# Second norm: inverse deviations of three token tiles made in one step behind the last unit's scaling, and their normalisation moved behind the loop over units

## The chip, the cores and the metric

One Trainium2 chip, of which the kernel uses one core. The metric is the device time in microseconds (us) of a run; the kernel before has a median of 427.91 us over 3 runs (426.51 to 429.72).

## The reference

The input is 16 images of 96 channels and 16 x 16 pixels. Three parts follow each other:

- a masked convolution from input to gates, then a recurrence over the 16 rows (per row a width-3 convolution of the hidden state, sigmoids, a cell `c = f*c + i*g`, `h = o*tanh(c)`), a 1x1 skip convolution and a residual;
- attention on the 256 tokens of each image, causal (6 heads of 16), on `_ln_t(t)`, with a residual: `t = t + attn(_ln_t(t))`;
- a mixture of 4 experts (96 to 384 to 96, exact gelu, top 2 of 4 by softmax) on `_ln_t(t)` of the new `t`, with a residual.

The norm before the experts is what the change touches. For each token over its 96 channels:

```
def _ln_t(v, eps=1e-05):
    m = jnp.mean(v, axis=-1, keepdims=True)
    s = jnp.var(v, axis=-1, keepdims=True)
    return (v - m) / jnp.sqrt(s + eps)
```

## The kernel before

**Tiling.** After the recurrence (the first 64 us or so) the tokens are worked through in 8 blocks (`NBLK`) of 512, each in 4 tiles (`SPB`) of 128 tokens. Attention of a block is cut into 10 units (`NU`), a unit being a few heads of one tile of queries. Units 0, 1 belong to tile 0 (three heads, 128 keys), units 2, 3, 4 to tile 1 (two heads, 256 keys), units 5, 6 to tile 2 (as tile 0), units 7, 8, 9 to tile 3 (as tile 1). `TILE_END` is [2, 5, 7, 10].

**A unit's way through the engines.** TensorE (PE) makes the scores in one of two banks `S` (`scores`, L1068 to L1073). VectorE (DVE) takes the row maximum (`row_max`, L792). ScalarE (ACT) makes the exponentials and their sums (`exps`, L598). DVE inverts the sums (`recip`, L798). GpSimd (POOL) multiplies the exponentials by them in place (`scale`, L453, one instruction for each head). PE transposes the result into the one bank `T` (`probs_t`, L1084), and ACT or DVE copies it out (`take_pt`, L502; ACT for units 1, 2, 4, 6, 8, 9, DVE for 0, 3, 5, 7). PE multiplies with the values into bank `A` (`values`, L1105) in slots 2, 5, 7 and behind the loop. `probs_t(u)` waits both for `scale(u)` and for the copy of unit u-1, since `T` is one bank.

**A tile's way after its last unit.** ACT copies `A` out (`heads_out`, L607), PE projects (`project_out`, L1111), DVE adds the residual and makes mean and variance (`attn_residual`, L805, L807, L809), POOL makes the inverse deviation (`rstd2`: an addition, L436, and a power of -1/2, L438), and DVE normalises (`normalize2`, L813). When all four tiles are there, PE transposes them (L1215), ACT and DVE split the result into two parts (`x2hi`, L639, and `x2lo`, L914), and the hidden layer of the experts runs (`expert_hidden`, L1142 to L1146, with the gelu on ACT, L644). The experts' second product of a block (`expert_out`, L1126) is spread as filling over the slots of the next block's attention (`FILL`), and DVE weighs it (`combine`, L870).

**Order.** Everything is written out by hand, and each engine executes its own list in order, with semaphores between them. One pass of the unit loop is slot j. On POOL, slot j holds `scale(n, j + 1)`; slot 2 also `rstd1(n + 1)` (the first norm of the next block, L430 and L432, all four tiles in one step); slots 3, 6 and 8 also `rstd2(n, 0)`, `rstd2(n, 1)`, `rstd2(n, 2)`, behind the scaling of that slot and so in front of `scale(n, 5)`, `scale(n, 8)` and, for tile 2, of nothing more. `rstd2(n, 3)`, `keep_t1`, `residual` and `x1_whole` follow behind the loop. On DVE, slot j holds `row_max(n, j + 2)`, `recip(n, j + 1)`, perhaps `take_pt`, `combine` and the first norm's work, `attn_residual` of tiles 0, 1, 2 in slots 3, 6, 8 and `normalize2` of the same tiles in slots 4, 7, 9. Behind the loop stand `combine(n - 1, 2)`, `attn_residual(n, 3)`, `q_rest`, `normalize2(n, 3)`, `k_rest`, `x2lo` and the rest. On PE, behind the loop: `project_q`, the values of units 7, 8, 9, `project_k`, `project_out(n, 3)`, nine parts of `expert_out`, then the transposes of L1215.

The first block (`first=True`) has no `expert_out` and no `combine` as filling; in some places PE runs matmuls there whose result nobody reads (`keep_clock`, L1008), but not in slots 3 to 9. The last block has no projection for a next block.

Of the kernel before, what the change touches and what calls it, by code (L numbers as in the profile page):

```python
# [23 lines left out]
ALU = mybir.AluOpType  # L24
# [14 lines left out]
SPB = 4  # L39
# [13 lines left out]
TILE_END = [1 + max(u for u, (a, t, _) in enumerate(UNITS) if 2 * a + t == s) for s in range(SPB)]  # L53
# [11 lines left out]
def hybrid_kernel(nc, x, w_input, w_state, b_skip, wq, wk, wv, wp, bp,  # L65
                  gate_w, gate_b, w1, b1, w2, b2, ident, ident_bf, causal_bf, lower, out):
    with ExitStack() as ctx:
        def sb(name, shape, dt=F32):
            return ctx.enter_context(nc.sbuf_tensor(name, shape, dt))
# [4 lines left out]
        def sem(name):  # L74
            return ctx.enter_context(nc.semaphore(name))
# [38 lines left out]
        nhalf = sb("nhalf", [128, SPB])  # L114
# [39 lines left out]
        mv2 = sb("mv2", [128, SPB, 2])  # L154
        ve2 = sb("ve2", [128, SPB])
        rs2 = sb("rs2", [128, SPB])
# [83 lines left out]
        ln2_aggr = sem("ln2_aggr")  # L240
# [6 lines left out]
        rs2_step = sem("rs2_step")  # L247
# [36 lines left out]
        def wait_alone(eng, semaphore, value):  # L284


            if not isinstance(value, int):
                value = eng.snap(eng.to_reg(value))
            eng.wait_ge(zeroed, N_ZEROED)
            eng.wait_ge(semaphore, value)  # L290
# [124 lines left out]
        @block.gpsimd  # L415
        def _(pool):
            nc.gpsimd.memset(h_pad[:], 0.0).then_inc(zeroed, 1)
            nc.gpsimd.memset(gate[:, :, 2], 0.0).then_inc(zeroed, 1)
            nc.gpsimd.memset(h_tok[:], 0.0).then_inc(zeroed, 1)
            nc.gpsimd.memset(as_f32(k_bd[:]), 0.0).then_inc(zeroed, 1)  # L420
            nc.gpsimd.memset(v_cur[:], 0.0).then_inc(zeroed, 1)
            nc.gpsimd.memset(nhalf[:], -0.5).then_inc(zeroed, 1)
            nc.gpsimd.memset(as_f32(ones2[:]), 0.0).then_inc(zeroed, 1)
            nc.gpsimd.memset(as_f32(b2hl[:]), 0.0).then_inc(zeroed, 1)
            pool.wait_ge(zeroed, N_ZEROED)

            def rstd1(n):

                wait_alone(pool, ln1_aggr, 4 * n + 4)
                nc.gpsimd.tensor_scalar(ve1[:], mv1[:, :, 1], 1e-5, None, ALU.add).then_inc(rs1_step, 1)  # L430
                pool.wait_ge(rs1_step, 2 * n + 1)
                nc.gpsimd.tensor_tensor(rs1[:], ve1[:], nhalf[:], ALU.pow).then_inc(rs1_step, 1)  # L432

            def rstd2(n, s):
                wait_alone(pool, ln2_aggr, 4 * n + s + 1)
                nc.gpsimd.tensor_scalar(ve2[:, s:s + 1], mv2[:, s, 1:2], 1e-5, None, ALU.add).then_inc(rs2_step, 1)  # L436
                pool.wait_ge(rs2_step, 8 * n + 2 * s + 1)
                nc.gpsimd.tensor_tensor(rs2[:, s:s + 1], ve2[:, s:s + 1], nhalf[:, 0:1], ALU.pow).then_inc(rs2_step, 1)  # L438

            def residual(n):  # L440

                pool.wait_ge(t0_done, n + 1)
                nc.gpsimd.tensor_tensor(tb[:], t0[:], bp_sb[:].unsqueeze(1).to_broadcast((128, SPB, C)),
                                        ALU.add).then_inc(tb_done, 1)

            def scale(n, u):

                wait_alone(pool, rden_done, NU * n + u + 1)
                _, t, _ = UNITS[u]
                nk = TT * (t + 1)  # L450
                for i in range(HG[t]):
                    p = p_sb[:, u % 3, i * nk:(i + 1) * nk]
                    last = nc.gpsimd.tensor_scalar(p, p, rden[:, u % 3, i:i + 1], 1.0, ALU.mult, ALU.mult)  # L453
                last.then_inc(scaled, 1)

            def x1_whole(n):

                wait_alone(pool, x1lo_done, n + 1)
                nc.gpsimd.tensor_tensor(x1f[:], as_f32(x1hi[:]), as_f32(x1lo[:]), ALU.add).then_inc(x1f_done, 1)

            def keep_t1(n, first):

                wait_alone(pool, t1_done, 4 * n + 4)
                if not first:
                    wait_alone(pool, comb, 16 * n)
                nc.gpsimd.tensor_copy(t1p[:], t1[:]).then_inc(t1p_done, 1)

            def body(n, first=False, last=False):
                scale(n, 0)
                for j in range(NU):  # L470
                    if j + 1 < NU:
                        scale(n, j + 1)
                    if j == EARLY_T0 + 1 and not last:
                        rstd1(n + 1)
                    for s in range(SPB - 1):
                        if j == TILE_END[s] + 1:
                            rstd2(n, s)
                rstd2(n, SPB - 1)
                keep_t1(n, first)
                if not last:  # L480
                    residual(n + 1)
                    x1_whole(n + 1)

            pool.wait_ge(w_in, 16 * N_WIN)
            rstd1(0)
            x1_whole(0)
            load_keys(nc.gpsimd, 0, 1, 0)
            residual(0)
            body(0, first=True)
            with pool.Fori(1, NBLK - 1) as n:  # L490
                body(n)
            body(NBLK - 1, last=True)
# [176 lines left out]
        def _(dve):  # L669
# [139 lines left out]
                V.bn_aggr(mv2[:, s], st2[:, s]).then_inc(ln2_aggr, 1)  # L809

            def normalize2(n, s):
                dve.wait_ge(rs2_step, 8 * n + 2 * s + 2)
                V.tensor_scalar(xh2[:, s], t1[:, s], mv2[:, s, 0:1], rs2[:, s:s + 1],  # L813
                                ALU.subtract, ALU.mult).then_inc(xh2_done, 1)

# [45 lines left out]
            def combine(n, s, first):  # L861

                dve.wait_ge(y_ready, 4 * n + s + 1)
                dve.wait_ge(t1p_done, n + 1)
                if s == 0 and not first:
                    dve.wait_ge(y_out, 16 * n)
                for e in range(E):
                    if e:
                        dve.wait_ge(comb, 16 * n + 4 * s + e)
                    V.scalar_tensor_tensor(y_sb[:, s], L2[s][:, e * C:(e + 1) * C], gw[:, s, e:e + 1],  # L870
                                           t1p[:, s] if e == 0 else y_sb[:, s], ALU.mult, ALU.add).then_inc(comb, 1)

            def body(n, first=False, second=False, last=False):
                if not first:
                    route(n - 1, 1)
                recip(n, 0)
                if first:
                    row_max(0, 1)
                else:
                    route(n - 1, 2)  # L880
                for j in range(NU):
                    if j + 2 < NU:
                        row_max(n, j + 2)
                    if j + 1 < NU:
                        recip(n, j + 1)
                    if j not in PT_ON_ACT:
                        take_pt(dve, n, j, first)
                    if j == EARLY_XT + 1 and not last:
                        x1_rest(n + 1)
                    if not first and j:  # L890
                        for s, c in out_parts(j - 1):
                            if c == NCH - 1:
                                combine(n - 1, s, second)
                    if not last:
                        if j == EARLY_T0 + 1:
                            norm1(n + 1)
                        if j == EARLY_T0 + 2:
                            normalize1(n + 1)
                    for s in range(SPB - 1):
                        if j == TILE_END[s] + 1:  # L900
                            attn_residual(n, s, first)
                        if j == TILE_END[s] + 2:
                            normalize2(n, s)
                if not first:
                    for s in range(sum(FILL[:-1]) // NCH, sum(FILL) // NCH):
                        combine(n - 1, s, second)
                attn_residual(n, SPB - 1)
                if not last:
                    q_rest(n + 1)
                normalize2(n, SPB - 1)  # L910
                if not last:
                    k_rest(n + 1)
                dve.wait_ge(x2hi_done, n + 1)
                V.tensor_tensor(x2lo[:], T[0:C, :], as_f32(x2hi[:]), ALU.subtract).then_inc(x2lo_done, 1)  # L914
                if not first:
                    for s in range(sum(FILL) // NCH, SPB):
                        combine(n - 1, s, second)
                route(n, 0)
                if not last:
                    row_max(n + 1, 0)  # L920
                    row_max(n + 1, 1)
# [410 lines left out]
```

## Time and profile before

| what | value |
|---|---|
| median of 3 runs | 427.91 us (426.51, 427.91, 429.72) |
| the profiled execution, its time | 431.65 us |
| its span, first to last instruction | 429.7 us |
| granted TensorE clock over the span | 0.987 of full |
| PE, busy | 404.0 us (94%), 3024 matmuls |
| ACT, busy | 267.1 us (62%) |
| DVE, busy | 248.3 us (58%) |
| POOL, busy | 147.6 us (34%) |

An engine's share is its busy time over the span. A steady block of 512 tokens takes 41.69 us (the same instruction of two blocks in a row: 190.54 and 232.23 us for the transposes of unit 8). Block 0 runs from about 85 us on, the last from about 380 us on.

### The profile page before, as it was taken

The page shows a single profiled execution, that of the slowest core. Times are in us where ns is not written, and L with a number is a line of the kernel's source. Part 1 is how long each engine was busy: PE and PEld are TensorE (multiplying, and loading weights), DVE is VectorE, ACT ScalarE, POOL GpSimd, SP SyncE. Part 2 cuts the span into 40 slices and gives each one's busy share as a digit, 9 for nine tenths or more (in the row PEclk, how much of TensorE's full clock was granted, in tenths as well). Part 3 has the DMA queues.
Part 4 walks back from the last instruction along what each step waited for, and adds up shares of the span by engine and source line. Part 5 has one row for each costly group of instructions (what it writes and reads, how often), then busy time and mean ns, then how long its engine had stood idle before and what let it go on. Part 6 is the DMA issues. An engine that isn't in the chain of part 4 may idle for free.

```text
span 429.7 us, 10320 instructions
## 1 busy us (share of the span) xinstructions
PE 404.0 (94%) x3024; PEld 332.1 (77%) x3024; DVE 248.3 (58%) x867; ACT 267.1 (62%) x766; POOL 147.6 (34%) x314
## 2 busy tenths in 40 slices
PE   7999998887999899989998999899989998999996
PEld 4988984555588788868886888789777887787786
DVE  1576774475328753866386548645864585367425
ACT  3566652465486658665865686567747764877380
POOL 6000002366305631563155315532642254236200
PEclk9899999998899999999999999999999999999999
DMA  7700000310111012101200220021002100210000
GB/s 177 177 0 0 0 2 19 83 29 2 43 36 36 2 46 53 30 0 50 55 23 0 54 55 21 0 61 49 18 0 64 46 0 8 76 27 3 7 13 20
DMA packets 16472, 14.87 MB, mean 35 GB/s; under 512 B 7586, under 2 KB 13588, under 8 KB 16452
## 3 DMA queue, kind: packets, MB, share of 16 engines
q1 hardware_dynamic: 14644, 13.74, 12.4%
q10 hardware_dynamic: 1616, 0.74, 0.7%
q8 instruction: 10, 0.16, 0.2%
q0 software_dynamic: 192, 0.15, 0.2%
q14 instruction: 10, 0.08, 0.1%
HBM read 3.80 MB, written 1.57 MB: 12 GB/s over the span
## 4 chain that ended last, share of the span: by engine, by line
PE 72%; DVE 9%; issue 7%; POOL 6%; ACT 3%; DMA 1%; ACTq 1%; SPq 1%; POOLq 0%; DVEq 0%
PE F L1126 14%; PE T L1084 6%; PE A L1105 5%; PE F L1142 5%; PE F L1146 4%; PE F L1143 4%; PE F L957 3%; POOL p_sb L453 3%; PE S L1068 3%; PE S L1070 2%; ACT p_sb L598 2%; PE F L967 2%; DVE xh L770 2%; PE F L968 2%; PE S L1073 2%
## 5 line engine op out<-in xcount | busy, mean ns | idle before, releaser
L453 POOL TENSOR_SCALAR p_sb<-p_sb,rden 128x128 f32<-128x128 f32 (+1 forms) x192 | 79.5, 429 | 115.3 <-DVE rden L798 113.1
L1126 PE MATMUL F<-w_sb,hid 128*128 128x96 f32 x768 | 98.8, 272 | 0.0
L1126 PEld LDWEIGHTS F<-w_sb,hid 128*128 128x128 f32 x768 | 96.1, 192 | 0.0
L598 ACT ACTIVATE p_sb<-S,nmax 128x128 f32<-128x128 f32 (+1 forms) x192 | 78.9, 424 | 11.4 <-DVE nmax L792 11.4
L792 DVE TENSOR_REDUCE nmax<-S 128x2 f32<-128x512 f32 (+1 forms) x80 | 50.6, 632 | 51.5 <-PE S L1073 51.2
L1084 PE MATMUL T<-id_sb,p_sb 128*128 128x128 f32 x288 | 48.1, 286 | 12.3 <-POOL p_sb L453 10.4
L502 ACT COPY pt_sb<-T 128x512 f32<-128x512 f32 (+1 forms) x48 | 26.5, 551 | 44.6 <-PE T L1084 44.6
L644 ACT ACTIVATE hid<-F,b_sb 128x512 f32<-128x512 f32 x72 | 49.4, 689 | 7.0 <-PE F L1146 6.3
L1084 PEld LDWEIGHTS T<-id_sb,p_sb 128*128 128x128 f32 x288 | 31.5, 144 | 21.9 <-POOL p_sb L453 17.7
L598 ACT ACTIVATION_READ_ACCUMULATOR p_sb<-S,nmax 128x1 f32 x192 | 39.7, 207 | 0.0
L1068 PE MATMUL S<-k_bd,q_st 96*128 96x384 f32 (+2 forms) x96 | 38.1, 404 | 1.5 <-ACT p_sb L598 1.1
L870 DVE SCALAR_TENSOR_TENSOR y_sb<-F,gw,y_sb 128x96 f32<-128x96 f32 x96 | 30.5, 318 | 3.4
L1070 PE MATMUL S<-k_bd,q_st 96*128 96x384 f32 (+2 forms) x96 | 31.7, 338 | 0.0
L1142 PE MATMUL F<-x2hi,w1hi 96*128 96x512 f32 x72 | 29.9, 415 | 1.4 <-ACT x2hi L639 0.8
L1146 PE MATMUL F<-x2lo,w1hi 96*128 96x512 f32 x72 | 29.2, 406 | 0.0
L1105 PE MATMUL A<-pt_sb,v_cur 128*32 128x128 f32 x576 | 28.9, 284 | 0.0
L1143 PE MATMUL F<-x2hi,w1lo 96*128 96x512 f32 x72 | 28.5, 396 | 0.0
L502 DVE COPY pt_sb<-T 128x384 f32<-128x384 f32 (+1 forms) x32 | 20.0, 624 | 11.4 <-PE T L1084 11.3
L1073 PE MATMUL S<-causal_sb,idb_sb 128*128 128x256 bf16 (+1 forms) x80 | 24.5, 306 | 0.0
L1105 PEld LDWEIGHTS A<-pt_sb,v_cur 128*32 128x32 f32 x576 | 20.0, 111 | 5.6 <-ACT pt_sb L502 3.0
L430 POOL TENSOR_SCALAR ve<-mv 128x4 f32<-128x4 f32 x8 | 1.9, 239 | 64.6 <-DVE mv L764 64.6
L436 POOL TENSOR_SCALAR ve<-mv 128x1 f32<-128x1 f32 x32 | 7.3, 227 | 46.0 <-DVE mv L809 45.3
(151 smaller groups left out, 789.3 us busy)
## 6 DMA issues: line engine op xcount, KB each, us to landing
k_bd<-k_cur SPq DMA_DIRECT2D x93, 32.0 KB, 2.0
q_st<-q_cur SPq DMA_DIRECT2D x28, 96.0 KB, 2.3
k_bd<-k_cur SPq DMA_DIRECT2D x93, 16.0 KB, 1.8
t_st<-t_cm SPq DMA_DIRECT2D x7, 192.0 KB, 2.5
out_y<-y_sb SPq DMA_DIRECT2D x7, 192.0 KB, 1.9
x_pad<-in_x SPq DMA_DIRECT2D x2, 612.0 KB, 7.4
w_sb<-in_w SPq DMA_DIRECT2D x1, 576.0 KB
hid<-in_w SPq DMA_DIRECT2D x1, 576.0 KB, 6.8
```

The lines of the kernel that those rows point to most:

```text
L453: last = nc.gpsimd.tensor_scalar(p, p, rden[:, u % 3, i:i + 1], 1.0, ALU.mult, ALU.mult)
L502: copy(pt_sb[:, u % NPT, 0:w], T[:, 0:w]).then_inc(pt_done, 1)
L598: last = nc.scalar.activation(p_sb[:, u % 3, i * nk:(i + 1) * nk], S[u % 2][:, i * nk:(i + 1) * nk], ACT.Exp, bias=nmax[:, u % 3, i:i + 1] ...
L644: nc.scalar.activation(hid[:, c, :], L1[c % 4][:], ACT.Gelu, bias=b1_sb[:, c:c + 1]).then_inc(gelu_done, 1)
L792: V.tensor_reduce(nmax[:, u % 3, 0:HG[t]], S[u % 2][:, 0:HG[t] * nk].rearrange("p (h k) -> p h k", k=nk), AX.X, ALU.max, negate=True).then ...
L1068: mm(d, q_st[:, g, ts], k_bd[:, a, 0, g, i0:i1, 0:nk], start=(3 * g + i0 == h0), stop=False, skip_group_check=True)
L1084: last = nc.tensor.transpose(T[:, i * TT:(i + 1) * TT], p_sb[:, u % 3, i * TT:(i + 1) * TT], id_sb[:])
L1105: last = mm(A[VW * (h % 3):VW * (h % 3) + VW, 0:TT], v, pt_sb[:, u % NPT, c0:c0 + TT], start=(kt == 0 and h < 3), stop=(kt == t and h >= 3 ...
L1126: last = mm(dst[:, e * C:(e + 1) * C], hid[:, c, s * TT:(s + 1) * TT], w2_sb[:, c], start=False, stop=(c == NCH - 1), skip_group_check=True)
L1142: mm(dst, w1hi[:, cs], x2hi[:], start=True, stop=False)
L1143: mm(dst, w1lo[:, cs], x2hi[:], start=False, stop=False)
L1146: mm(dst, w1hi[:, cs], x2lo[:], start=False, stop=True).then_inc(hid_ready, 1)
```

## The change

`rstd2` takes a range of tiles instead of one. It is called twice for a block, both times behind the loop over units: for tiles 0 to 2 in one addition and one power of 128 x 3 elements, then for tile 3. The three calls in the loop are gone. It waits for the statistics of the last tile of its range. `rs2_step` counts 4 in a block instead of 8. On DVE `normalize2` of tiles 0, 1 and 2 leaves slots 4, 7 and 9 and stands in a row behind the loop, behind `combine(n - 1, 2)` and in front of `attn_residual(n, 3)`.

```diff
-            def rstd2(n, s):
-                wait_alone(pool, ln2_aggr, 4 * n + s + 1)
-                nc.gpsimd.tensor_scalar(ve2[:, s:s + 1], mv2[:, s, 1:2], 1e-5, None, ALU.add).then_inc(rs2_step, 1)
-                pool.wait_ge(rs2_step, 8 * n + 2 * s + 1)
-                nc.gpsimd.tensor_tensor(rs2[:, s:s + 1], ve2[:, s:s + 1], nhalf[:, 0:1], ALU.pow).then_inc(rs2_step, 1)
+            def rstd2(n, s0, s1):
+
+                wait_alone(pool, ln2_aggr, 4 * n + s1)
+                nc.gpsimd.tensor_scalar(ve2[:, s0:s1], mv2[:, s0:s1, 1], 1e-5, None, ALU.add).then_inc(rs2_step, 1)
+                pool.wait_ge(rs2_step, 4 * n + (3 if s0 else 1))
+                nc.gpsimd.tensor_tensor(rs2[:, s0:s1], ve2[:, s0:s1], nhalf[:, s0:s1], ALU.pow).then_inc(rs2_step, 1)
...
                         rstd1(n + 1)
-                    for s in range(SPB - 1):
-                        if j == TILE_END[s] + 1:
-                            rstd2(n, s)
-                rstd2(n, SPB - 1)
+                rstd2(n, 0, SPB - 1)
+                rstd2(n, SPB - 1, SPB)
                 keep_t1(n, first)
...
             def normalize2(n, s):
-                dve.wait_ge(rs2_step, 8 * n + 2 * s + 2)
+                dve.wait_ge(rs2_step, 4 * n + (4 if s == SPB - 1 else 2))
...
                             attn_residual(n, s, first)
-                        if j == TILE_END[s] + 2:
-                            normalize2(n, s)
                 if not first:
                     for s in range(sum(FILL[:-1]) // NCH, sum(FILL) // NCH):
                         combine(n - 1, s, second)
+                for s in range(SPB - 1):
+                    normalize2(n, s)
                 attn_residual(n, SPB - 1)
```

## Rows read from the trace of the kernel before

**Rows 1.** The page, part 1: busy time, share of the span, instructions.
```profile
PE 404.0 (94%) x3024; PEld 332.1 (77%) x3024; DVE 248.3 (58%) x867; ACT 267.1 (62%) x766; POOL 147.6 (34%) x314
```
**Rows 2.** Waits by line: waiter, releaser, us in total, times, longest us.
```profile
PE T L1084 <- POOL p_sb L453: 10.4, 10, 1.4
...
PE T L1215 <- DVE xh L813: 1.1, 7, 0.2
```
**Rows 3.** The tile rs: times in ns (least/median/most), first and last start.
```profile
L438 POOL TENSOR_TENSOR rs<-ve,nhalf x32: 567/569/579, 96.9 to 402.9; 128x1 f32<-128x1 f32 x32
...
L432 POOL TENSOR_TENSOR rs<-ve,nhalf x8: 1042/1043/1052, 69.9 to 345.8; 128x4 f32<-128x4 f32 x8
```
**Rows 4.** Timeline of POOL, a steady block (start, us, instruction, idle before).
```profile
225.31 1.09 POOL L453 TENSOR_SCALAR p_sb<-p_sb,rden 128x128 f32<-128x128 f32 x3
...
229.23 0.93 POOL L453 TENSOR_SCALAR p_sb<-p_sb,rden 128x256 f32<-128x256 f32 x2 [1.06 <-DVE rden L798]
230.24 0.23 POOL L436 TENSOR_SCALAR ve<-mv 128x1 f32<-128x1 f32 x1
...
231.22 1.87 POOL L453 TENSOR_SCALAR p_sb<-p_sb,rden 128x256 f32<-128x256 f32 x4
```
**Rows 5.** Timeline of the other engines, same block, units 5 to 9.
```profile
226.65 0.31 PEld L1084 LDWEIGHTS T<-id_sb,p_sb 128*128 128x128 f32 x3 [0.20 <-POOL p_sb L453]
...
228.91 0.15 DVE L798 RECIPROCAL rden<-den 128x2 f32<-128x2 f32 x1
...
230.39 0.15 DVE L798 RECIPROCAL rden<-den 128x2 f32<-128x2 f32 x1
...
230.98 0.69 DVE L502 COPY pt_sb<-T 128x512 f32<-128x512 f32 x1 [0.44 <-PE T L1084]
...
231.59 0.32 DVE L813 TENSOR_SCALAR xh<-t,mv,rs 128x96 f32<-128x96 f32 x1
...
232.23 0.66 PE L1084 MATMUL T<-id_sb,p_sb 128*128 128x128 f32 x4 [1.09 <-POOL p_sb L453]
...
232.93 0.59 ACT L502 COPY pt_sb<-T 128x512 f32<-128x512 f32 x1 [1.25 <-PE T L1084]
...
233.62 0.42 PEld L1084 LDWEIGHTS T<-id_sb,p_sb 128*128 128x128 f32 x4 [0.26 <-issue]
```
**Rows 6.** Timeline, same block, behind the loop over units.
```profile
233.78 0.18 DVE L809 BATCH_NORM_AGGREGATE mv<-st 128x2 f32<-128x6 f32 x1
...
235.63 1.02 DVE L870 SCALAR_TENSOR_TENSOR y_sb<-F,gw,y_sb 128x96 f32<-128x96 f32 x3
...
237.09 0.26 DVE L805 TENSOR_TENSOR t<-M,tb 128x96 f32<-128x96 f32 x1 [0.44 <-PE M L1111]
...
239.39 0.64 PE L1215 MATMUL T<-id_sb,xh 128*96 128x128 f32 x4 [0.15 <-DVE xh L813]
```
**Rows 7.** Timeline of the last block, units 7 and 8.
```profile
396.22 0.69 DVE L502 COPY pt_sb<-T 128x512 f32<-128x512 f32 x1 [0.48 <-PE T L1084]
...
397.23 0.66 PE L1084 MATMUL T<-id_sb,p_sb 128*128 128x128 f32 x4 [0.84 <-POOL p_sb L453]
```
**Rows 8.** Timeline of the first block, units 5 to 8.
```profile
96.73 0.17 DVE L798 RECIPROCAL rden<-den 128x3 f32<-128x3 f32 x1
...
97.53 2.19 POOL L453 TENSOR_SCALAR p_sb<-p_sb,rden 128x128 f32<-128x128 f32 x6
...
98.71 0.55 PE L1084 MATMUL T<-id_sb,p_sb 128*128 128x128 f32 x3 [0.59 <-POOL p_sb L453]
...
102.97 0.69 DVE L502 COPY pt_sb<-T 128x512 f32<-128x512 f32 x1 [0.47 <-PE T L1084]
...
104.35 1.07 PE L1084 MATMUL T<-id_sb,p_sb 128*128 128x128 f32 x4 [1.43 <-POOL p_sb L453]
```
**Rows 9.** Windows, PE: stretch, length, busy (count), granted clock, DMA share, GB/s.
```profile
104.35:111.31 6.96, 6.56 (x40) 0.51 0.00 0
232.23:236.48 4.25, 4.12 (x44) 1.00 0.00 0
```

## The prediction

> **What bounds the kernel now.** I read the busy shares first, then the waits by line, then the timeline of one steady block (190.54 to 232.23 us between the same transposes, 41.69 us), and last the first and the last block. PE is busy for 94% of the span [rows 1], so only its idle time can be won, and its own list must be followed to see what a shift is worth. The waits name one place: the transposes of the scaled probabilities waited 10 times for POOL's scaling, 10.4 us together [rows 2]. In the timeline of a steady block that is unit 8: PE stands still for 1.09 us until 232.23 [rows 5]; the six steady blocks show this pause at 1.09 or 1.10 us. The last block has 0.84 us [rows 7], the first 1.43 us at unit 8 and 0.59 us at unit 5 [rows 8]. The reader should see what POOL does just before: it ends the scaling of unit 7 at 230.16 (229.23 + 0.93), makes the inverse deviation of tile 1 from 230.24 on, and starts the scaling of unit 8 at 231.22 [rows 4], although its reciprocal was done at 230.54 [rows 5]. The small step on one column stands in front of the scaling that PE waits for.
>
> **Part 1, removed from POOL's loop.** One inverse deviation holds POOL from 230.24 to 231.22, 0.98 us from start to start [rows 4]. The two durations alone are 0.23 [rows 4] and 0.57 [rows 3], 0.80 us. The Trainium skill ("Perfetto Trace Analysis", on the profiler's boundary for GPSIMD) advises timing POOL by the spacing of starts; by durations the step would be 0.18 us cheaper. The next terms use starts, and do not need that advice.
>
> Without the step, scaling 8 starts as late behind its reciprocal as scaling 7 does: that reciprocal ended at 229.06, the scaling started at 229.23, 0.17 later [rows 4, 5]. So 230.54 + 0.17 = 230.71, the pair takes 0.93 as in unit 7, and PE follows 0.08 us behind (232.23 against 231.22 + 0.93 = 232.15): 231.72. But the transposes also need bank T, which DVE's copy of unit 7 leaves at 231.67 (230.98 + 0.69); PE needed 0.10 us behind such a copy for unit 9 (233.62 against 232.93 + 0.59) [rows 5]. That gives 231.77, and the gain is 232.23 - 231.77 = **0.46 us**. What is late next is the copy of unit 7, so more than 0.46 can't come from here; the lower bound is 0 if something not seen holds unit 8.
>
> Is it kept? From unit 8 on PE's list is a chain: unit 9's transposes follow the copy of unit 8 by 0.10 us, then come the projections and values without a pause of note, until the residual of tile 3 at 237.09 and the transposes of the norm at 239.39 [rows 6]. All move together, and with them the query and key transfers that DVE releases there. Scaling 9 would run from 231.64 to 232.57, and unit 9's transposes would be due at 233.16: no new wait. Six steady blocks: 6 x 0.46 = **2.8 us**.
>
> In front of unit 5 the step also goes. There the scaling ended at 226.40, PE's transposes began only at 226.65 [rows 4, 5], three times the 0.08 seen behind unit 8, so PE itself set that moment; steady unit 5 counts 0. The last block: the copy of unit 7 ends at 396.91, plus 0.10 is 397.01 against 397.23 [rows 7]: **0.2 us**. The first block has no filling, so both steps cost. Unit 5: reciprocal done at 96.90, plus 0.17 is 97.07 against 97.53, 0.46 us, of which PE waited 0.59 [rows 8]; everything to unit 8 follows that. Unit 8: copy done at 103.66, plus 0.10 is 103.76 against 104.35, 0.59 us more [rows 8]. Together **1.05 us**.
>
> **Part 2, the same work in one step.** A power of four columns takes 1.043 us, of one 0.569 [rows 3]; three lie between, evenly 0.885 us. Bounds 0.57 and 1.04. It follows the statistics of tile 2 at 233.96 [rows 6] and stands behind scaling 9, which is over by then. Taking 0.16 us to start and 0.31 for the addition (0.98 less 0.67 for the power with its gap), the result is there at about 235.3. Behind it on POOL waits only tile 3's own step, whose statistics come some 2.6 us later. Cost on the path: 0, covered by PE's values and projections.
>
> **Part 3, three normalisations on DVE.** 0.32 us each [rows 5], some 0.95 in a row. DVE now ends the weighing of tile 2 at 236.65 and then idles 0.44 until the projection of tile 3 at 237.09 [rows 6]. Tile 2's normalisation no longer stands in front of that weighing with its wait for POOL, so the weighing (four instructions, three of them 1.02 us [rows 6], 1.4 us with the first) starts at 233.96 and ends near 235.4, the three normalisations near 236.35, and some 0.75 us stay before 237.09; the shift of part 1 moves all of these alike. Cost 0; upper bound, were none of this room there, 0.5 us in a block (236.65 + 0.95 against 237.09). Taken out of slots 4 and 7, two normalisations free DVE by 0.25 us each, in front of row maxima and reciprocals; DVE idles 0.44 us in front of the copy of unit 7 [rows 5], so I count 0, bound 0.05 us a block from the reciprocal of unit 9.
>
> **The clock.** From 104.35 to 111.31 the granted clock is 0.51, the lower of the two levels (1.2 GHz), after PE stood still for 1.43 us [rows 8, 9]; the same way through the list takes 4.25 us in a steady block at 2.4 GHz [rows 9], although that has the filling as well. The low stretch costs about 2.7 us. The change shortens the pauses in front of it from 0.59 and 1.43 us by 0.46 and 0.59. In a steady block a pause of 1.09 us does not lower the clock. What it gives: 0 if the clock falls anyway, 2.7 if never.
>
> The Trainium skill ("TensorE: Matmul & The Clock Gate", the part on HAM oscillation) says that pauses of PE make the gate lower its clock and that keeping it supplied holds the clock up; by that rule alone the first block would keep 2.4 GHz, and the profile of before agrees as far as the fall goes: 0.51 behind the pause of 1.43 us.
>
> **Sum.** 2.8 + 0.2 + 1.05 = 4.0 us without the clock. The profiled execution took 431.65 us (span 429.7 and 1.95 around it), 3.7 above the median; with the clock kept up it would read 431.65 - 4.0 - 2.7 = 424.9. The runs shown spread over 3.2 us, about what the low stretch costs, so I take the highest to have it whole, the lowest not at all, and the median 427.91 - 426.51 = 1.4 us of it. Forecast 427.91 - 4.0 - 1.4 = **422.5 us**.
>
> **Rivals.**
> - *Clock as before.* The waits go, the low stretch comes as often: 427.91 - 4.0 = 423.9. For it: the pauses get shorter but don't vanish. Chance 0.25.
> - *Clock counts whole.* All runs of before had the low stretch, none after: 427.91 - 6.7 = 421.2. For it: the profiled one has it. Against: its time lies above all runs shown. Chance 0.13.
> - *Hidden anyway.* Another release sets unit 8 or the gain is eaten behind the loop, where PE still waits for the last normalisation 0.15 us [rows 6] (1.1 us in all [rows 2]); half of the 4.0 stays: 425.9. Chance 0.13.
> - *The end is late (slower).* The batched step delays the residual of tile 3. It decides once the inverse deviations are later than 237.09 - 0.95 = 236.14, that is, a batch of over 2.0 us from 234.12. As three single steps it would be 3 x 0.98 = 2.94, done at 237.06, and the residual 0.92 us late in 8 blocks, 7.4 us: 431.3 with the gain of part 1, 435.3 if that fails too. Against it stands the four-column power of 1.043 us [rows 3]. Chance 0.05.
>
> The forecast has 0.44. **The numbers.** One per cent is 4.3 us, about what this kernel's measurement can tell from none; the limit is 423.6. Faster by more: nearly all of the forecast's case and the whole-clock case, a third of the clock-as-before case: 0.6. Within: the rest of that, the hidden case and the slower one with part 1's gain: 0.36. Slower: 0.04. The range goes from 420.7, just below the whole-clock case with 0.05 us a block more, to 426.0, which takes in the half gain.
>
> **What would show it.** Right: in a steady block POOL's scaling of unit 8 starts 0.17 us behind its reciprocal, PE's pause there falls from 1.09 to about 0.6 us and now ends 0.10 us behind DVE's copy of unit 7; the block takes 41.2 us instead of 41.7; one power of 128x3 lasts near 0.89 us; the residual of tile 3 still waits for PE's projection, by about 0.75 us. In the first block the pause at unit 8 is below 0.9 us and no stretch of low clock follows. Wrong: a block still takes 41.7, a wait of the residual's on DVE's own normalisations, or the low clock at another place of the first block.

## The result, and the profile after

The changed kernel takes **424.14 us** (median of 11 runs, 422.45 to 425.27) against 428.10 for the kernel before in runs beside it (11, 426.46 to 432.96): a ratio of 0.9892, 95% interval 0.9867 to 0.9917. The forecast was 422.5 us, in a range of 420.7 to 426.0. It is faster by 1.1%, as forecast, and by 3.96 us of medians where 5.4 had been expected.

The page of the changed kernel, busy time and share of the span (421.1 us; the profiled execution took 423.02 us). It answers to [rows 1]:
```profile
PE 399.7 (95%) x3024; PEld 328.1 (78%) x3024; DVE 249.4 (59%) x867; ACT 266.8 (63%) x766; POOL 137.2 (33%) x282
```
POOL has 32 instructions fewer: two of the three inverse deviations of each of 8 blocks, two instructions each. PE's busy time fell by 4.3 us too although its work is the same: that is the low clock that this execution does not have (granted clock 1.000 over the span, 0.987 before).

Its waits by line (waiter, releaser, us in total, times, longest), against [rows 2]:
```profile
PE T L1083 <- DVE pt_sb L501: 5.6, 8, 0.9
...
PE T L1083 <- POOL p_sb L454: 1.7, 3, 0.9
PE T L1214 <- DVE xh L812: 1.2, 7, 0.2
```
Of 10.4 us behind POOL's scaling 1.7 are left, and 5.6 us stand now behind a releaser that was not in the list for this line: DVE's copy of the unit before.

The tile rs of the changed kernel, against [rows 3] (ns, first and last start):
```profile
L439 POOL TENSOR_TENSOR rs<-ve,nhalf x16: 579/730/887, 103.4 to 394.2; 128x3 f32<-128x3 f32 x8, 128x1 f32<-128x1 f32 x8
```

The timeline of POOL in a steady block, against [rows 4]:
```profile
222.56 0.94 POOL L454 TENSOR_SCALAR p_sb<-p_sb,rden 128x256 f32<-128x256 f32 x2 [1.31 <-DVE rden L797]
224.04 0.93 POOL L454 TENSOR_SCALAR p_sb<-p_sb,rden 128x256 f32<-128x256 f32 x2 [0.55 <-DVE rden L797]
225.37 0.93 POOL L454 TENSOR_SCALAR p_sb<-p_sb,rden 128x256 f32<-128x256 f32 x2 [0.39 <-DVE rden L797]
227.01 0.24 POOL L437 TENSOR_SCALAR ve<-mv 128x3 f32<-128x3 f32 x1 [0.71 <-DVE mv L808]
227.34 0.88 POOL L439 TENSOR_TENSOR rs<-ve,nhalf 128x3 f32<-128x3 f32 x1
```
Three scalings (units 7, 8, 9), each started by its reciprocal, and then the addition and the power of three columns. The other engines in the same block, against [rows 5, 6]:
```profile
223.72 0.16 DVE L797 RECIPROCAL rden<-den 128x2 f32<-128x2 f32 x1
...
224.31 0.69 DVE L501 COPY pt_sb<-T 128x512 f32<-128x512 f32 x1 [0.44 <-PE T L1083]
...
225.15 0.63 PE L1083 MATMUL T<-id_sb,p_sb 128*128 128x128 f32 x4 [0.68 <-DVE pt_sb L501]
...
226.55 0.63 PE L1083 MATMUL T<-id_sb,p_sb 128*128 128x128 f32 x4
...
226.67 0.18 DVE L808 BATCH_NORM_AGGREGATE mv<-st 128x2 f32<-128x6 f32 x1
...
227.20 1.02 DVE L869 SCALAR_TENSOR_TENSOR y_sb<-F,gw,y_sb 128x96 f32<-128x96 f32 x3
228.25 0.81 DVE L812 TENSOR_SCALAR xh<-t,mv,rs 128x96 f32<-128x96 f32 x3
229.99 0.26 DVE L804 TENSOR_TENSOR t<-M,tb 128x96 f32<-128x96 f32 x1 [0.93 <-PE M L1110]
```
The scaling of unit 8 is done at 224.97 (224.04 + 0.93), but PE goes on only at 225.15, 0.15 us behind the end of the copy (225.00). The power of three columns and DVE's weighing both end at 228.22, the three normalisations at 229.06, and DVE idles 0.93 us before the residual of tile 3.

The first block, PE's transposes of units 7, 8 and 9, against [rows 8]:
```profile
99.66 0.66 PE L1083 MATMUL T<-id_sb,p_sb 128*128 128x128 f32 x4
101.19 0.63 PE L1083 MATMUL T<-id_sb,p_sb 128*128 128x128 f32 x4 [0.88 <-DVE pt_sb L501]
...
102.63 0.66 PE L1083 MATMUL T<-id_sb,p_sb 128*128 128x128 f32 x4 [0.61 <-POOL p_sb L454]
```
Windows of PE in the changed kernel (stretch, length, busy with count, granted clock, DMA share, GB/s):
```profile
10.00:15.00 5.00, 4.34 (x26) 1.00 1.09 240
15.00:20.00 5.00, 5.00 (x34) 1.00 0.59 163
98.00:104.00 6.00, 4.37 (x37) 1.00 0.00 1
104.00:111.00 7.00, 6.24 (x53) 1.00 0.19 54
```
The same windows of the kernel before, near the start:
```profile
10.00:15.00 5.00, 4.33 (x18) 0.73 1.09 238
15.00:20.00 5.00, 5.00 (x31) 0.93 0.61 172
```
The low stretch of the first block is gone in this execution, but so is one at 10 to 20 us, ahead of anything that the change touches. So the two spans differ by more than the change is worth. To divide the 8.6 us (429.7 against 421.1) I take four marks: the start, the transposes of unit 0 of the first block (87.29 before, 85.20 after), and the first and the last transposes of the norm. In the kernel before:
```profile
114.39 0.42 PE L1215 MATMUL T<-id_sb,xh 128*96 128x128 f32 x2
...
403.85 0.31 PE L1215 MATMUL T<-id_sb,xh 128*96 128x128 f32 x1 [0.20 <-DVE xh L813]
```
and in the changed one, with the second block's between them:
```profile
108.57 0.31 PE L1214 MATMUL T<-id_sb,xh 128*96 128x128 f32 x1
...
149.80 0.31 PE L1214 MATMUL T<-id_sb,xh 128*96 128x128 f32 x1 [0.17 <-DVE xh L812]
...
395.24 0.53 PE L1214 MATMUL T<-id_sb,xh 128*96 128x128 f32 x3 [0.17 <-DVE xh L812]
```
That gives 2.09 us in the start, 27.10 - 23.37 = 3.73 in the first block, 289.46 - 286.67 = 2.79 in the seven that follow, and nothing in the tail (25.85 and 25.86). The first is not the change's. One steady block, between the same marks, takes 41.23 us (149.80 - 108.57) instead of 41.65; over all six it is 41.23 to 41.26 against 41.65 to 41.71.

### The profile page after: what moved, and what is told of

The parts are those of the page before. It is cut to its first block, busy times and chain, and to the rows that moved or that the text cites. A ratio compares the mean times of both kernels' runs of the same rounds, so it can differ in the third digit from the quotient of the medians.

```text
span 421.1 us, 10222 instructions
## 1 busy us (share of the span) xinstructions
PE 399.7 (95%) x3024; PEld 328.1 (78%) x3024; DVE 249.4 (59%) x867; ACT 266.8 (63%) x766; POOL 137.2 (33%) x282
## 4 chain that ended last, share of the span: by engine, by line
PE 82%; DVE 6%; issue 3%; POOL 3%; ACT 2%; DMA 1%; ACTq 1%; SPq 1%; POOLq 0%; DVEq 0%
PE F L1125 16%; PE T L1083 8%; PE A L1104 6%; PE F L1141 5%; PE F L1145 4%; PE S L1067 4%; PE F L1142 4%; PE S L1069 3%; PE F L956 3%; PE S L1072 2%; PE F L966 2%; PE M L1110 2%; PE F L967 2%; DVE pt_sb L501 2%; PE S L972 1%
## 5 line engine op out<-in xcount | busy, mean ns | idle before, releaser
L1083 PE MATMUL T<-id_sb,p_sb 128*128 128x128 f32 x288 | 46.6, 280 | 8.8 <-DVE pt_sb L501 5.6
L1104 PE MATMUL A<-pt_sb,v_cur 128*32 128x128 f32 x576 | 28.0, 278 | 0.0
L1067 PEld LDWEIGHTS S<-k_bd,q_st 96*128 96x128 f32 x96 | 18.2, 190 | 3.6 <-ACT p_sb L597 2.4
```

Source lines behind the costliest of these rows:

```text
L1067: mm(d, q_st[:, g, ts], k_bd[:, a, 0, g, i0:i1, 0:nk], start=(3 * g + i0 == h0), stop=False, skip_group_check=True)
L1083: last = nc.tensor.transpose(T[:, i * TT:(i + 1) * TT], p_sb[:, u % 3, i * TT:(i + 1) * TT], id_sb[:])
L1104: last = mm(A[VW * (h % 3):VW * (h % 3) + VW, 0:TT], v, pt_sb[:, u % NPT, c0:c0 + TT], start=(kt == 0 and h < 3), stop=(kt == t and h >= 3 ...
```

## The experiments

Twelve kernels were run. "At full clock" below means those runs whose granted clock, over the whole run, was at least 0.998 of the higher level. Of 73 runs of the kernel before (a 74th, at 433.48 us, is left out), 27 were such (mean 427.16 us), 24 had 0.993 to 0.997 (428.54) and 22 less (430.29). They come in four sets beside the experiments, whose runs at full clock have means of 427.07 to 427.31. Of 11 runs of the changed kernel 5 were at full clock (422.82), 6 at 0.994 to 0.996 (424.53) and none below. So at full clock the change is worth 4.34 us. The marks of the traces give 3.78 of it, as shown under before_filled; the other half microsecond is not explained. I compare on this footing beside the ratio, because a low stretch costs as much as the differences looked for.

**norm_moved_only.** Half of the change: the kernel before with only the normalisations moved. (The other half can't run by itself: the normalisations must follow POOL's steps.)
```
-                        if j == TILE_END[s] + 2:
-                            normalize2(n, s)
...
+                for s in range(SPB - 1):
+                    normalize2(n, s)
                 attn_residual(n, SPB - 1)
```


> The DVE half of the change alone: the kernel before, with the normalisations of tiles 0 to 2 moved behind the loop, while POOL makes the inverse deviations one by one in its slots as before. Theory (POOL's single step in front of the scaling of unit 8 is what PE pays for, 0.42 us in a steady block by the trace of the changed kernel): nothing moves, the pause in front of unit 8 stays at 1.05 to 1.10 us, median within 0.5 us of the kernel before. Rival (the normalisations in DVE's slots, in front of row maxima and reciprocals, were the cause): the pause falls to about 0.68 us and 3 to 4 us are won.


Measured: 427.58 us (12 runs), ratio 0.9968 [0.9943, 0.9993]; at full clock 426.84, 0.32 better than before. By medians it is 0.94 under the kernel before beside it (428.52), more than the 0.5 allowed; 7 of its 12 runs were at full clock, against 10 of 29. PE at unit 8 of a steady block:
```profile
229.70 0.66 PE L1084 MATMUL T<-id_sb,p_sb 128*128 128x128 f32 x4 [1.07 <-POOL p_sb L453]
```
1.07 us where it was 1.09, and blocks of 41.59 to 41.75 us: nearly all of the gain comes from POOL's order.

**singles_behind.** The changed kernel, both moves in it, but with four single steps on POOL behind the loop. Against the changed kernel:
```
-                rstd2(n, 0, SPB - 1)
-                rstd2(n, SPB - 1, SPB)
+                for s in range(SPB):
+                    rstd2(n, s)
```


> As the changed kernel, but with four single inverse deviations behind the loop instead of one of three tiles and one of one. Theory (my slower rival's mechanism, with its point of decision): POOL starts at 227.0 in the block of the changed kernel's trace, three single steps of 0.98 us end at 229.9, the third normalisation ends at about 230.2, and the residual of tile 3, due at 229.99, is some 0.25 us late in seven blocks and 0.8 us in the last: 2 to 2.5 us more than the changed kernel, still 2 us less than before. Rival (there is room for any order behind the loop): the same time as the changed kernel.


Measured: 423.13 us (6 runs), ratio 0.9876 [0.9849, 0.9903]; at full clock 422.90 against 422.82. The expected loss did not come. POOL in a steady block:
```profile
228.87 0.23 POOL L436 TENSOR_SCALAR ve<-mv 128x1 f32<-128x1 f32 x1
...
229.73 0.22 POOL L436 TENSOR_SCALAR ve<-mv 128x1 f32<-128x1 f32 x1
...
230.58 0.22 POOL L436 TENSOR_SCALAR ve<-mv 128x1 f32<-128x1 f32 x1
230.89 0.57 POOL L438 TENSOR_TENSOR rs<-ve,nhalf 128x1 f32<-128x1 f32 x1
```
Two assumptions failed. A single step takes 0.855 us from start to start in a row, not the 0.98 read between a step and a scaling. And the first step starts right behind the scaling of unit 9 (over at 228.78), at 228.87, ahead of the statistics of tile 2 (229.16 + 0.18 = 229.34), for which the batch must wait. All three are done at 231.46, and DVE still idled 0.65 us before the residual of tile 3. So the gain comes from **where** the steps stand; that they are made together is worth nothing here (a steady block takes 41.18 to 41.20 us, against 41.23 to 41.26 with the batch).

**before_filled.** The clock by itself: the kernel before, with matmuls in the first block that nobody reads.
```
+                    if first and j >= 3:
+                        keep_clock({3: 0, 4: 4, 5: 2, 6: 0, 7: 1, 8: 7, 9: 3}[j])
                     probs_t(n, j, first)
```


> The kernel before, with matmuls whose result nobody reads in the first block only, in front of the transposes of units 4, 5, 7, 8 and 9 (4, 2, 1, 7 and 3 of them, about 0.155 us each), where PE stood idle. Theory (the low clock of the first block comes from those pauses and costs up to 2.7 us in a run that has it): no stretch of low clock between 90 and 115 us in the profile, median 1 to 2.5 us lower than the kernel before, and less spread. Rival (low clock comes mainly elsewhere or is not in most runs): median unchanged within 0.5 us.


Measured: 427.20 us (12 runs; before, beside it, 428.52), ratio 0.9971 [0.995, 0.9991]; 9 of the 12 at full clock, none below 0.993. Windows of PE in its first block:
```profile
100.00:105.00 5.00, 4.69 (x38) 1.00 0.00 2
105.00:110.00 5.00, 4.92 (x48) 1.00 0.00 0
```
Without a change to POOL or DVE the low stretch is gone, where [rows 9] has 0.51. From unit 4's transposes to the norm's, this block takes 16.27 us, against 19.00 before and 15.28 in the changed kernel. So in the profiled execution the clock made 2.73 us of the first block, and the shorter waits 0.99. With the 2.79 of the later blocks, the waits make 3.78 us.

**fill_moved.** Two weight-stream parts from slot 0 to slot 8, to fill the pause left at unit 8.
```
-FILL = [16, 3, 3, 2, 3, 3, 2, 1, 1, 2]
+FILL = [14, 3, 3, 2, 3, 3, 2, 1, 3, 2]
```


> The changed kernel with 14 instead of 16 parts of the experts' second product in slot 0 and 3 instead of 1 in slot 8, where PE still waits 0.68 us for the copy of unit 7. Theory (PE is the bound, and only its idle time counts): two parts take 0.53 us of the pause; if slots 0 to 4 can do with less filling, a block is 0.3 to 0.5 us shorter, 2 to 3.7 us in all against the changed kernel. Rival (slots 0 to 4 then wait for the scalings of units 1 and 4 instead, which had 0.3 and 0.1 us of room): the pause only moves, the time stays within 0.7 us of the changed kernel.


Measured: 430.07 us (12 runs), ratio 1.0047 [1.0021, 1.0073]; at full clock 429.38, 6.6 us worse than the changed kernel. Neither theory had that. A steady block (now about 42.15 us), DVE and then POOL:
```profile
225.47 1.02 DVE L869 SCALAR_TENSOR_TENSOR y_sb<-F,gw,y_sb 128x96 f32<-128x96 f32 x3
226.41 0.68 DVE L791 TENSOR_REDUCE nmax<-S 128x2 f32<-128x512 f32 x1
```
```profile
227.33 0.93 POOL L454 TENSOR_SCALAR p_sb<-p_sb,rden 128x256 f32<-128x256 f32 x2 [3.23 <-DVE rden L797]
```
The list also sets the slot in which DVE weighs a finished tile. With 14 in slot 0, tile 1 is complete one slot later, its weighing stands in front of a row maximum, and all that hangs on that is late: POOL idles 3.23 us and PE 1.13 us at unit 7. The parts in front of unit 8 were never tested by this run.

**fill_one_late** and **fill_two_late.** The same question without that side effect: one and two parts from slot 4 to slot 8, so that every tile ends in its old slot. The diff is the first one's; the second has 1 in slot 4 and 3 in slot 8.
```
-FILL = [16, 3, 3, 2, 3, 3, 2, 1, 1, 2]
+FILL = [16, 3, 3, 2, 2, 3, 2, 1, 2, 2]
```


> The changed kernel with one part of the experts' second product (two matmuls, 0.27 us) moved from slot 4 to slot 8, which leaves the slots in which the tiles of that product end as they are. Theory (the pause in front of unit 8 now follows from the copy of unit 7, this from unit 7's transposes, and these from PE's own list, so work moved from in front of units 5 to 7 into the pause is won): 0.27 us in a steady block, pause at unit 8 from 0.68 to about 0.4 us, 1.5 to 2 us in all against the changed kernel. Rival (the scalings of units 5 to 7 do not come earlier): the pause moves to units 6 and 7, and nothing is won.

> As the one before with two parts moved from slot 4 to slot 8. Theory: 0.4 to 0.53 us in a steady block, 2.5 to 3.7 us in all; at unit 5 the scaling ends 0.5 us before PE gets there, so the second part may wait at units 5 or 6. Rival: no more than with one part.


Measured: 423.52 us (6), ratio 0.9889 [0.9853, 0.9924], and 423.93 us (6), 0.989 [0.985, 0.993]; at full clock 423.25 and 422.72. PE of the second, units 4 and 8:
```profile
217.99 0.66 PE L1083 MATMUL T<-id_sb,p_sb 128*128 128x128 f32 x4 [0.24 <-POOL p_sb L454]
...
226.84 0.63 PE L1083 MATMUL T<-id_sb,p_sb 128*128 128x128 f32 x4 [0.23 <-DVE pt_sb L501]
```
The pause at unit 8 falls from 0.68 to 0.23, but unit 4 now waits: its scaling stands behind the four-column power (1.04 us) on POOL. The fill was cover there: from unit 3's transposes to unit 4's it is 2.23 us, against 2.26 with both parts in between. Steady blocks of 41.20 to 41.24 and 41.23 to 41.27 us (the first of the second kernel 41.33), against 41.23 to 41.26: nothing won.

The first block of these two kernels and of fill_moved is that of the changed kernel, and two of their profiles have the low clock in it. fill_one_late, then fill_moved:
```profile
105.00:110.00 5.00, 5.00 (x39) 0.66 0.00 0
```
```profile
105.00:110.00 5.00, 5.00 (x44) 0.85 0.00 0
```
Their pauses at units 8 and 9 are those of the changed kernel (0.87 and 0.61 us), yet from unit 4's transposes to the norm's they take 16.82 us, 1.54 more than its 15.28. So the low stretch of the first block can still come after the change; the one profile of the changed kernel didn't have it.

**after_filled.** The changed kernel with the unread matmuls.
```
+                    if first and j >= 3:
+                        keep_clock({3: 0, 4: 4, 5: 0, 6: 0, 7: 1, 8: 4, 9: 3}[j])
```


> The changed kernel with unread matmuls in the first block only, in front of the transposes of units 4, 7, 8 and 9 (4, 1, 4 and 3 of them). The kernel before, filled in the same way, lost its low clock in the first block (granted clock 0.999 or more in 9 of 12 runs against 10 of 29). Theory (the changed kernel still has the low stretch of the first block in a part of its runs: 6 of 11 had a granted clock of 0.994 to 0.996): these runs become fewer, median 0.5 to 1.3 us under the changed kernel, near 423. Rival (those runs have their low clock in the start, which no matmul here touches): as the changed kernel, and the same share of such runs.


Measured: 424.07 us (6 runs), ratio 0.9904 [0.9867, 0.9941]; 3 of 6 at full clock (423.01), 3 at 0.995 to 0.996. The gain of 0.5 to 1.3 us did not come, and the share of runs below full clock is about that of the changed kernel alone (6 of 11). So a part of its low clock probably lies elsewhere than in the first block; six runs can't say how much. The profiles show both places: at 10 to 20 us in singles_behind, fill_one_late and fill_two_late (granted 0.66 to 0.88), in the first block in fill_one_late and fill_moved.

**room_used.** The end made late on purpose: two unread four-column powers in front of the batch.
```
+                if not s0:
+                    for i in range(2):
+                        nc.gpsimd.tensor_tensor(scr[:, i], ve1[:], nhalf[:], ALU.pow).then_inc(rs2_step, 1)
+                        pool.wait_ge(rs2_step, 6 * n + 2 + i)
```


> The changed kernel with two further powers of four columns (about 1.05 us each with the step between, results unread) in front of the power of three columns behind the loop. Theory (the slower rival's mechanism with the room measured in the trace of the changed kernel: DVE idles 0.93 us in front of the residual of tile 3 in a steady block, 0.34 us in the last): 2.2 us more on POOL are 1.3 us late in each of six or seven blocks and 1.8 us in the last, 9 to 11 us more than the changed kernel, about 434. Rival (something else sets the end of a block, so lateness there is hidden in part): less than 5 us more.


Measured: 437.18 to 453.35 us in four runs (clocks 0.946 to 0.984), too far apart for a ratio; the profiled one took 450.78. Its waits, and windows of PE:
```profile
PE T L1219 <- DVE xh L817: 10.8, 8, 1.9
```
```profile
115.00:120.00 5.00, 5.00 (x16) 0.50 0.16 37
205.00:210.00 5.00, 5.00 (x16) 0.50 0.16 36
375.00:380.00 5.00, 5.00 (x18) 0.50 0.23 59
420.00:425.00 5.00, 5.00 (x16) 0.50 0.11 39
```
The lateness itself is near what was expected: the batch's power starts 2.20 us behind the first of the extra ones, 0.93 of it is room, 1.27 is left; in the second block PE waits 1.32 instead of 0.17 at the norm's transposes, 1.15 more. What was not expected is that the clock then fell in four of the eight blocks. With the waits alone, 10.8 against 1.2 us, this kernel would take about 434.

**tile0_in_loop.** Tile 0's inverse deviation back in POOL's loop, in front of unit 5.
```
+                    if j == TILE_END[0] + 1:
+                        rstd2(n, 0, 1)
+                rstd2(n, 1, SPB - 1)
```


> The changed kernel with the inverse deviation of tile 0 back in its slot, in front of the scaling of unit 5; tiles 1 and 2 in one step behind the loop. Theory (only the step in front of unit 8 cost anything in a steady block; the one in front of unit 5 counts in the first block alone): steady block 41.2 us as in the changed kernel, the transposes of unit 5 in the first block 0.4 to 0.5 us later, 0.5 us more in all, plus at times a low clock there. Rival (each step in the loop costs about the same): half of the 0.42 us of a steady block is lost again, 1.5 us or more.


Measured: 424.93 us (10 runs), ratio 0.9904 [0.9874, 0.9934]; at full clock 424.18, 1.4 worse than the changed kernel. A steady block takes 41.21 to 41.25 us: in front of unit 5 the step costs nothing there. The first block, units 5 and 8:
```profile
98.22 0.55 PE L1085 MATMUL T<-id_sb,p_sb 128*128 128x128 f32 x3 [0.55 <-POOL p_sb L454]
...
103.51 0.66 PE L1085 MATMUL T<-id_sb,p_sb 128*128 128x128 f32 x4 [1.08 <-POOL p_sb L454]
```
The loss is in this block, since the seven that follow take as long as in the changed kernel (286.63 against 286.67). From unit 4's transposes it is 0.47 us at unit 5 and 0.66 at unit 8, which waits longer as well (1.08 against 0.88): its scaling starts 0.53 us behind its reciprocal, and the profile shows no reason. The rest of the 1.4 is not explained by pauses; this profile also had the low clock from 105 to 110 us (0.67), but the 1.4 is between runs at full clock.

**recip_first.** The reciprocal ahead of the row maximum on DVE from slot 5 on, so that scalings start sooner.
```
+                    if j >= 5 and j + 1 < NU:
+                        recip(n, j + 1)
                     if j + 2 < NU:
                         row_max(n, j + 2)
```


> The changed kernel with DVE's reciprocal of a unit's sums ahead of the row maximum of the next but one in slots 5 to 8, not behind it; so the scalings of units 6, 7 and 8 can start up to 0.5 us earlier. Theory (the pause in front of unit 8 is now set by the copy of unit 7 out of bank T, not by the scaling): scaling 8 ends well before that copy, and the transposes of unit 8 come no earlier, at most 0.1 us a block. Rival (the scaling still sets it, the two being 0.1 us apart): up to 0.3 us a block, 2 us in all.


Measured: 425.99 us (12 runs), ratio 0.9941 [0.991, 0.9972]; at full clock 425.21, 2.4 worse than the changed kernel; most steady blocks take 41.28 to 41.40 us, one 41.88. Units 8 and 9:
```profile
230.98 0.63 PE L1085 MATMUL T<-id_sb,p_sb 128*128 128x128 f32 x4 [0.68 <-DVE pt_sb L501]
...
232.49 0.66 PE L1085 MATMUL T<-id_sb,p_sb 128*128 128x128 f32 x4 [0.24 <-POOL p_sb L454]
```
Unit 8 does not move although its scaling is over at 230.56, 0.42 us before PE starts, where that was 0.18 in the changed kernel: the copy sets it, not the scaling. Unit 9 waits anew (in the first block 1.19 us instead of 0.61), because the reciprocal of unit 8 waited for its exponentials and held the row maximum of unit 9 behind it.

**recip_first_fill** and **recip56_fill.** The same with two parts of the fill moved from slot 5 to slot 8, where the pause is; in the second, whose diff this is, the reciprocal is first only in slots 5 and 6.
```
-FILL = [16, 3, 3, 2, 3, 3, 2, 1, 1, 2]
+FILL = [16, 3, 3, 2, 3, 1, 2, 1, 3, 2]
...
+                    if j in (5, 6):
+                        recip(n, j + 1)
```


> As recip_first, and two parts of the experts' second product moved from slot 5 to slot 8. Theory (units 5, 6, 7 follow PE's list once their scalings are early, unit 8 follows unit 7 by its copy; so 0.53 us of work less in front of unit 5 pulls the whole chain ahead, and the work fills the pause): steady block 40.7 us against 41.2, pause at unit 8 from 0.68 to 0.2 us, 3 to 3.7 us less than the changed kernel, about 420.5. Rival (the scalings of units 6 or 7 or their exponentials don't come early enough): the pause only moves to unit 6 or 7, as it moved to unit 4 where the parts were taken from slot 4; less than 1 us.

> As recip_first_fill, but the reciprocal goes ahead of the row maximum in slots 5 and 6 alone; in slot 7 the row maximum of unit 9 stands first again. In recip_first_fill the reciprocal of unit 8 waited for its exponentials and held that row maximum, so unit 9 was late: PE waited 0.24 us for its scaling in each block. Theory (the order of slot 7 cost that): the pause in front of unit 9 is gone, the one of unit 8 stays at 0.2 us, steady block 40.7 us, 2.5 to 3.5 us less than the changed kernel, about 421. Rival (the reciprocal of unit 8 behind the row maximum makes scaling 8 late instead): a pause of 0.2 us more at unit 8, nothing won against recip_first_fill.


Measured: 423.03 us (6 runs), ratio 0.9877 [0.9822, 0.9932], and **421.95 us** (6 runs, 421.67 to 422.93), 0.9853 [0.9808, 0.9897]. In the first, unit 8 waits 0.23 us but unit 9 0.21 to 0.26, and a steady block takes 40.93 to 41.05; at full clock (3 runs, 422.15) it gains 0.7 us on the changed kernel, not the 3 or more of the theory. Units 8 and 9 of the second:
```profile
225.30 0.63 PE L1085 MATMUL T<-id_sb,p_sb 128*128 128x128 f32 x4 [0.23 <-DVE pt_sb L501]
...
226.69 0.63 PE L1085 MATMUL T<-id_sb,p_sb 128*128 128x128 f32 x4
```
Unit 8 waits 0.23, unit 9 not at all; a block takes 40.78 us instead of 41.23, and the way from the first to the last transposes of the norm 283.75 instead of 286.67. The intervals of this ratio and of the changed kernel's overlap, so that it beats the changed kernel rests on that trace, 2.9 us, and on the comparison by clock. None of its six runs was at full clock (all 0.996, mean 422.14); the changed kernel's six at 0.994 to 0.996 have 424.53, 2.4 us more. The medians show 2.2. Its profile has a low stretch in the first block (0.83 from 100 to 110 us).

## Why the prediction was right, and where it was off

**The main term held, mechanism and size.** The pause at unit 8 fell from 1.09 to 0.68 us and ends behind DVE's copy; the forecast said 0.46 gained and 0.42 came (41.65 to 41.23). From the end of unit 8's reciprocal to its scaling it is 0.16 us (223.88 to 224.04), against 0.17 taken. From the copy's end to PE's start it is 0.15 where unit 9 had shown 0.10: that accounts for the missing 0.04. norm_moved_only and singles_behind show that POOL's order does it, and recip_first that an earlier scaling gives nothing more at that place. The seven blocks with the last gave 2.79 of 3.0.

**Unit 5** was counted at nothing in a steady block; tile0_in_loop puts the step back there and pays nothing (41.21 to 41.25). In the first block both steps were counted, 1.05 us. Against before_filled, whose clock was kept up, unit 8 comes 1.06 us earlier behind unit 4 (7.90 against 8.96), and 0.99 is left at the norm's transposes.

**The batch and the normalisations at nothing.** The three-column power takes 0.88 us (0.885 taken); the result is there 1.37 us behind the statistics of tile 2, at 228.22 (1.34 taken). The room before the residual of tile 3 is 0.93 us, not 0.75, mainly since three normalisations in a row take 0.81 us and not 0.95. room_used shows that it is real room: an excess of 1.27 came out as 1.15.

**The mis-sized term is the clock in the sum**, "the median 427.91 - 426.51 = 1.4 us of it". That the low stretch of the first block cost 2.7 us in the profiled execution was right (2.73). Over the runs of the kernel before, low clock costs 1.4 us (428.56 on the mean of 73, against 427.16 at full clock), just the figure taken; but that holds the stretches at 10 to 20 us as well, and the forecast knew of none there, so this agreement is in part luck. Wrong was the silent assumption that the changed kernel would have none. Six of its 11 runs are below full clock, and the mean of all is 0.93 over that at full clock. Of the 1.4 only about 0.5 came back by means, and by medians nothing: 3.96 us in all, less than the 4.34 at full clock. Two things stood against it. The profiled execution of before had two low stretches, and I had queried only the one at the change; the one at 10 to 20 us, which [rows 9] leave out, comes and goes with either kernel. And the one in the first block still comes at times behind the shortened pauses (fill_one_late, fill_moved), at 1.54 us instead of 2.73. The forecast was 1.64 us too low: the clock took 0.4 away where 1.4 was counted as a gain (1.8 short), the gain at full clock is 4.3 where 4.0 was counted (0.3 over), and 0.19 is there because the kernel before read 428.10 beside it, not 427.91. The 0.3 over belongs to the half microsecond that the traces don't explain, so it is luck that it covers a part of the clock's error. The rival "clock as before", 423.9, lies nearest to 424.14. What decides in a given run whether the start or the first block keeps its clock stays open; for the start it was not tried.

The Trainium skill ("TensorE: Matmul & The Clock Gate", the part on HAM oscillation) holds PE's pauses responsible for low clock; its case is a kernel whose TensorE waits for DMA for longer than it works between the waits. The prediction stretched that to pauses of about 1 us. before_filled agrees for the first block: with the pauses filled, the granted clock stayed at 1.00. By the size of a single pause the traces don't agree: in room_used one of 1.32 us, ending at 156.75, was followed by a granted clock of 1.00 up to 170, another of 1.32 us, ending at 199.43, by 0.50, and the same pauses of 0.87 and 0.61 us in the first block were followed by 1.00 in one profile and by 0.66 in another.

**The slower rival** was priced wrong from both sides. Its condition could hardly come about: single steps need not wait for tile 2 (singles_behind, 422.90 at full clock, where the rival had 431.3). But were it met, its price would probably be higher than 7.4 us, since in room_used such waits came with the low clock in four of eight blocks.

**Hidden anyway** is refuted by the block of 41.23 us.

## What to carry to other kernels

The price of a small instruction is what stands behind it in its engine's queue: look for one off the critical path that stands in front of one on it, and move it, before thinking of making it shorter or fewer. Before pricing the move, read the next releaser of the same wait, because it caps the gain; a following experiment has to move that one, and each moved piece drags along whatever is placed by the same list. A low-clock stretch in one profile must be set against how often it comes in the runs, and looked for over the whole span, not only at the change.

## What the runs showed of the hardware

- A step of addition and power on one column takes 0.98 us from start to start in front of a scaling, but 0.855 in a row of its like. The powers took 0.57, 0.88 and 1.04 us for one, three and four columns. The Trainium skill ("Perfetto Trace Analysis", on the profiler's boundary for GPSIMD) advises to time such steps by their starts; here the spacing also depends on what comes next, so that of the same pair has to be taken.
- Three normalisations of 0.32 us each take 0.81 us together.
- The runs of the kernel before fall into groups by granted clock, with means 1.4 and 1.7 us apart (427.16, 428.54, 430.29).
- Pauses of PE of 0.88 and 0.61 us in the first block left the clock at 1.00 in the changed kernel, but the same pauses (0.87 and 0.61) were followed by 0.66 in fill_one_late; waits of 1.0 to 1.9 us at the blocks' ends were followed by 0.50 in four of eight blocks (room_used). The size of a pause does not decide by itself whether the clock falls.
